# A kernel of eight fused layers on one core: the keys of the second full attention are computed inside the first cross attention, kept in DRAM and read back

## What is computed

```
x = x + L0_xattn(ln(x), ctx, mask)      # channels against channels, 16 heads of 8
x = x + L0_ffn(ln(x))                   # 8 experts, top 2
x = x + L1_xattn(ln(x), ctx)            # 16 heads of 16
x = x + L1_ffn(ln(x))                   # quantised, 256 -> 1024 -> 256
x = x + L2_xattn(ln(x), ctx)            # 16 heads of 128: q = ln(x) Wq, k = ctx Wk, v = ctx Wv
x = x + L2_ffn(ln(x))                   # LoRA experts
x = x + L3_xattn(ln(x), ctx, mask)      # memory readout
x = x + L3_ffn(ln(x))                   # grouped attention and 8 experts
```

## Time and profile before

| | us |
|---|---|
| median of three timed runs | 1279.91 |
| lowest and highest | 1278.62, 1280.27 |
| span of the profiled execution, first to last instruction | 1275.9 |
| what lies around the span, median less span | 4.0 |
| TensorE busy in the profile | 1085.1 |
| VectorE, ScalarE, GpSimd busy | 704.5, 503.4, 319.7 |

### The profile page before, as it was taken

The page is one execution under the profiler, slowest core; times in us unless marked ns, Lnnn a source line. Parts: engine busy times, 40 slices in busy tenths (PEclk is TensorE's granted clock), DMA queues, the critical chain, the costliest instruction groups (busy, mean ns, idle before and its releaser), DMA issues.

```text
span 1275.9 us, 20612 instructions
## 1 busy us (share of the span) xinstructions
PE 1085.1 (85%) x7154; PEld 830.8 (65%) x7170; DVE 704.5 (55%) x1700; ACT 503.4 (39%) x1785; POOL 319.7 (25%) x440
## 2 busy tenths in 40 slices
PE   1788886999996788799999999996788999984784
PEld 0355444899995566588888888884555666653463
DVE  5777756212223788854554455555656666665334
ACT  0165561233231466644333333342445555542121
POOL 5544211122322355510000000002222222210562
PEclk9699996899997799999999999998989999997797
DMA  6443207899882070000000000040000000000785
GB/s 185 133 129 110 84 32 237 301 327 334 315 322 79 10 256 1 2 28 20 1 1 1 1 1 1 34 133 1 1 1 9 5 6 5 5 4 24 238 250 177
DMA packets 59731, 121.31 MB, mean 95 GB/s; under 512 B 9049, under 2 KB 37481, under 8 KB 53713
## 3 DMA queue, kind: packets, MB, share of 16 engines
q1 hardware_dynamic: 52217, 106.62, 25.0%
q0 software_dynamic: 4416, 12.06, 2.8%
q10 hardware_dynamic: 2996, 1.32, 0.4%
HBM read 107.29 MB, written 12.49 MB: 94 GB/s over the span
## 4 chain that ended last, share of the span: by engine, by line
PE 60%; DVE 17%; issue 8%; ACT 7%; DMA 4%; POOL 2%; SPq 1%; another core or an unknown queue 1%; ACTq 0%; DVEq 0%; POOLq 0%
PE P L858 6%; PE P L868 6%; PE P L1789 4%; PE P L1782 4%; PE P L1834 4%; PE P L1798 4%; ACT big L2213 3%; DVE small L480 2%; PE P L1927 2%; PE P L1807 2%; PE P L1822 2%; PE P L1933 2%; PE P L1978 2%; ACT big L2181 2%; PE P L341 1%
## 5 line engine op out<-in xcount | busy, mean ns | idle before, releaser
L139 POOL TENSOR_TENSOR lrs<-lve,mhalf 128x1 f32<-128x1 f32 x64 | 36.6, 572 | 364.5 <-DVE lve L130 332.4
L480 DVE TENSOR_REDUCE small<-P 128x2 f32<-128x512 f32 x128 | 83.3, 681 | 38.9 <-PE P L305 38.2
L2124 ACT ACTIVATE big<-P,small 128x128 f32<-128x128 f32 x128 | 45.2, 366 | 145.0 <-DVE small L2304 145.0
L897 ACT ACTIVATE big<-P,big 128x128 f32<-128x128 f32 x184 | 52.5, 368 | 125.3 <-PE P L858 112.4
L556 ACT ACTIVATE big<-P 128x512 f32<-128x512 f32 x128 | 72.0, 598 | 58.6 <-PE P L323 53.6
L858 PE MATMUL P<-big 128*128 128x128 f32 x736 | 88.2, 279 | 0.1
L858 PEld LDWEIGHTS P<-big 128*128 128x128 f32 x736 | 86.1, 196 | 1.0 <-DMA big<-b_w 0.5
L868 PE MATMUL P<-big 128*128 128x256 f32 x368 | 83.1, 379 | 0.0
L305 PE MATMUL P<-big 90*128 90x256 bf16 x256 | 54.9, 303 | 32.9 <-DMA big<-scr_qk 17.5
L2295 DVE COPY big<-P 128x512 f32<-128x512 f32 x32 | 22.1, 692 | 107.2 <-PE P L1798 107.2
L999 DVE COPY big<-P 128x256 f32<-128x256 f32 x23 | 9.8, 425 | 125.3 <-PE P L868 125.3
(11 more groups left out here) (388 smaller groups left out, 2584.2 us busy)
## 6 DMA issues: line engine op xcount, KB each, us to landing
big<-b_w SPq DMA_DIRECT2D x23, 1028.0 KB
big<-b_w SPq DMA_DIRECT2D x23, 1024.0 KB
big<-scr_qk SPq DMA_DIRECT2D x96, 96.0 KB
big<-i_wgu SPq DMA_DIRECT2D x23, 352.0 KB
big<-moe_y SPq DMA_DIRECT2D x16, 256.0 KB, 4.2
big<-i_wd SPq DMA_DIRECT2D x23, 176.0 KB
scr_qk<-big SPq DMA_DIRECT2D x8, 384.0 KB
moe_x<-XN SPq DMA_DIRECT2D x16, 128.0 KB
```

Source lines behind the costliest of these rows:

```text
L480: dve.tensor_reduce(negM[:, h, :], P[:, h % 2, :].rearrange("p (c s) -> p c s", c=2), AX.X, ALU.max, negate=True).then_inc(a_max, 1)
```

## The change

The 32 parts of `k = ctx Wk` (128 head features by 512 tokens, four rows at once) are made by `key_part` in the first cross attention: parts 0 to 7 before its first step, parts 8 to 19 as halves of 256 columns in steps 0 to 23, parts 20 to 31 as halves in rows 2 to 7 at heads 5, 8, 11 and 14. ScalarE copies each part to SBUF (`key_take`) and stores it from its own queue (`key_store`, 256 KB in runs of 512 bytes). In the second full attention `keys4` and the copy to `e_k` are gone; each row's keys (1 MB) are read from DRAM into one of two buffers (`key_row`), and `e_q` has two buffers. Loads are rearranged for it: half of the context transposed and the first key weights come ahead of the remaining rows of `x` and `ctx`; `s0_behind` sends loads and mask rows behind the store of a row's queries and keys; the ACT queue carries rows 4 to 7 of `x` and one group of key weights. Loads of the grouped attention's weights wait for other counts, and semaphores are reused with an offset (a count of `e_ld` from 16 instead of 0, and the like), which are left out below.

```
@@ -210,6 +210,44 @@
+        k_wts = big1[:, 12288:16384].rearrange("p (g k n) -> p g k n", g=4, k=KD)
+        k_out = [XNT[:, s // 2, 512 * (s % 2):512 * (s % 2) + 512] for s in range(4)]
+        KEYS = nc.dram_tensor("keys_t", (B, 128, 4, 4, T), F32, kind="Internal").ap()
+        KP, K0, K1 = 32, 8, 20
+        def key_place(p):
+            g, rest = divmod(p, 8)
+            return g, rest // 4, rest % 4
+        def key_bank(p):
+            return 2 + p % 2 if p < K1 else 5
+        def key_weights(eng, g):
+            eng.dma_start(k_wts[:, g], e_wk.rearrange("(k p) n -> p k n", p=128)[:, :, 512 * g:512 * g + 512]
+                          ).then_inc(k_w[g], 16)
+        def key_take(act, p):
+            act.wait_ge(k_pe, p + 1)
+            if p >= 4:
+                act.wait_ge(k_st[p % 4], 16 * (p // 4))
+            act.activation(k_out[p % 4], P[:, key_bank(p), :], ACT.Copy).then_inc(k_ev, 1)
+        def key_store(act, p):
+            g, r, j = key_place(p)
+            act.wait_ge(k_ev, p + 1)
+            act.dma_start(KEYS[4 * r:4 * r + 4, :, g, j].rearrange("b p t -> p b t"),
+                          k_out[p % 4].rearrange("p (b t) -> p b t", b=4)).then_inc(k_st[p % 4], 16)
+        def late_pair(n, h):
+            if 2 <= n < B and h in (5, 8, 11, 14):
+                at = (5, 8, 11, 14).index(h)
+                return K1 + 2 * (n - 2) + at // 2, at % 2
+            return None
...
+            sp.dma_start(X[:, 2:4, :], x_cbt[:, 2:4, :]).then_inc(ld_x, 16)
+            ctx_t = ctxT.rearrange("(k p) n -> p k n", p=128)
+            sp.dma_start(CT[:, :, 0:512], ctx_t[:, :, 0:512]).then_inc(k_w[0], 16)
+            key_weights(sp, 0)
+            sp.dma_start(CT[:, :, 512:NT], ctx_t[:, :, 512:NT]).then_inc(k_ct, 16)
             sp.dma_start(idf[:, :], ident).then_inc(ld_id, 16)
-            sp.dma_start(X[:, 2:8, :], x_cbt[:, 2:8, :]).then_inc(ld_x, 16)
-            sp.dma_start(CX[:, 2:8, :], ctx_cbt[:, 2:8, :]).then_inc(ld_c, 16)
-            for dst, src in ((wvT, a_wvT), (bvb, rows(a_bv)), (tmT, maskT), (selm, a_sel),
-                             (TMf[:, 2 * D:], rows(mask_row[:, 2 * D:]))):
+            sp.dma_start(CX[:, 2:4, :], ctx_cbt[:, 2:4, :]).then_inc(ld_c, 16)
+            for dst, src in ((wvT, a_wvT), (bvb, rows(a_bv)), (tmT, maskT)):
...
+        def s0_behind(sp, n):
+            TMf = TM.rearrange("p b d -> p (b d)")
+            if n == 1:
+                sp.dma_start(TMf[:, 2 * D:], rows(mask.rearrange("b d -> (b d)").rearrange("(a n) -> a n", a=1)[:, 2 * D:])
+                             ).then_inc(a_ldm, 16)
+                sp.wait_ge(a_exd, 32)
+            if n in (1, 2):
+                for half in range(2):
+                    s0_extra(sp, n, half)
+            if n == 1:
+                key_weights(sp, 2)
+            if n == 2:
+                sp.dma_start(CX[:, 4:8, :], ctx.rearrange("b c t -> c b t")[:, 4:8, :]).then_inc(ld_c2, 16)
+                sp.dma_start(selm, a_sel).then_inc(a_ldm, 16)
+                key_weights(sp, 3)
...
+            def key_part(p, lo, hi):
+                g, r, j = key_place(p)
+                if lo == 0:
+                    if p % 8 == 0:
+                        pe.wait_ge(k_w[g], 32 if g == 0 else 16)
+                    if p == 4:
+                        pe.wait_ge(k_ct, 16)
+                    if p >= K1:
+                        pe.wait_ge(k_ev, p)
+                    elif p >= 2:
+                        pe.wait_ge(k_ev, p - 1)
+                for k in range(KD):
+                    t = pe.matmul(P[:, key_bank(p), lo:hi], k_wts[:, g, k, 128 * j:128 * j + 128],
+                                  CT[:, k, 512 * r + lo:512 * r + hi], start=(k == 0), stop=(k == KD - 1))
+                if hi == 512:
+                    t.then_inc(k_pe, 1)
             project(0)
             project(1)
+            for p in range(K0):
+                key_part(p, 0, 512)
             for step in range(STEPS):
                 n, h = divmod(step, H)
                 if n < B:
@@ -381,6 +469,13 @@
                 m, g = divmod(step - LEAD, H)
                 if 0 <= m < B:
                     turned(m, g)
+                if step < LEAD:
+                    key_part(K0 + step // 2, D * (step % 2), D * (step % 2) + D)
+                if late_pair(n, h) is not None:
+                    p, u = late_pair(n, h)
+                    if n + 2 < B and h == 5:
+                        pe.wait_ge(a_qb, n + 3)
+                    key_part(p, D * u, D * u + D)
...
+            key_take(act, 0)
+            key_store(act, 0)
+            act.dma_start(X[:, 4:8, :], x.rearrange("b c t -> c b t")[:, 4:8, :]).then_inc(ld_x2, 16)
+            key_take(act, 1)
+            key_store(act, 1)
+            key_weights(act, 1)
             act.wait_ge(a_exd, 32)
-            for n in range(3):
-                for half in range(2):
-                    s0_extra(act, n, half)
+            for p in range(2, K0):
+                if p in (2, 4):
+                    s0_extra(act, 0, p // 2 - 1)
+                key_take(act, p)
+                key_store(act, p)
...
+                if step < LEAD and step % 2:
+                    key_take(act, K0 + step // 2)
+                    key_store(act, K0 + step // 2)
                 if h == 3 and n + 2 < B:
                     queries_keys(n + 2)
                 if h == 4 and 0 < n <= B:
                     max_rows(n - 1)
                 if h == 7 and n < B:
                     values(n)
+                if 2 <= n < B and h in (9, 15):
+                    key_take(act, late_pair(n, h - 1)[0])
+                if 2 <= n < B and h == 11:
+                    key_store(act, late_pair(n, 8)[0])
+                if 3 <= n <= B and h == 1:
+                    key_store(act, late_pair(n - 1, 14)[0])
...
+        def key_row(sp, b):
+            if b >= 2:
+                sp.wait_ge(e_s, 4 * (b - 2) + 4)
+            sp.dma_start(e_kr[b % 2], KEYS[b]).then_inc(k_rd[b % 2], 16)
         def s4_sp(sp):
             sp.wait_ge(xn_ready, 3 * B)
-            for w, src in enumerate((e_wq, e_wk)):
-                for g in range(4):
-                    sp.dma_start(e_wqk[:, g, w], src.rearrange("(k p) n -> p k n", p=128)[:, :, 512 * g:512 * g + 512]
-                                 ).then_inc(e_ld, 16)
+            for signal in k_st:
+                sp.wait_ge(signal, 16 * KP // 4)
+            wq4 = e_wq.rearrange("(k p) n -> p k n", p=128)
+            sp.dma_start(e_wqs[:, 0], wq4[:, :, 0:512]).then_inc(e_ld, 16)
+            key_row(sp, 0)
+            for g in range(1, 4):
+                sp.dma_start(e_wqs[:, g], wq4[:, :, 512 * g:512 * g + 512]).then_inc(e_ld, 16)
             for g in range(4):
                 sp.dma_start(e_wvs[:, g], e_wv.rearrange("(k p) n -> p k n", p=128)[:, :, 512 * g:512 * g + 512]
                              ).then_inc(e_ld, 16)
             sp.dma_start(e_wos, e_wo.rearrange("(h p) d -> p h d", p=128)).then_inc(e_ld, 16)
+            key_row(sp, 1)
...
-            def keys4(m):
-                b, g = divmod(m, 4)
-                for j in range(4):
-                    for k in range(KD):
-                        t = pe.matmul(P[:, 1, j * T:j * T + T], e_wqk[:, g, 1, k, j * 128:j * 128 + 128],
-                                      CT[:, k, b * T:b * T + T], start=(k == 0), stop=(k == KD - 1))
...
             def scores4(m):
                 pe.wait_ge(e_qkT, m + 1)
+                b, g = divmod(m, 4)
+                if g == 0:
+                    pe.wait_ge(k_rd[b % 2], KRD0 + 16 * (b // 2) + 16)
                 if m >= 2:
                     pe.wait_ge(e_exp, m - 1)
                 for j in range(4):
-                    t = pe.matmul(P[:, 3 + m % 2, j * T:j * T + T], e_q[:, j, :], e_k[:, j, :], start=True, stop=True)
+                    t = pe.matmul(P[:, 3 + m % 2, j * T:j * T + T], e_q[m % 2][:, j, :], e_kr[b % 2][:, g, j, :],
+                                  start=True, stop=True)
                 t.then_inc(e_s, 1)
...
             def copy_qk4(m):
                 act.wait_ge(e_qk, m + 1)
-                if m > 0:
-                    act.wait_ge(e_s, m)
-                act.activation(e_q.rearrange("p j t -> p (j t)"), P[:, 0, :], ACT.Copy)
-                act.activation(e_k.rearrange("p j t -> p (j t)"), P[:, 1, :], ACT.Copy).then_inc(e_qkT, 1)
+                if m >= 2:
+                    act.wait_ge(e_s, m - 1)
+                act.activation(e_q[m % 2].rearrange("p j t -> p (j t)"), P[:, 0, :], ACT.Copy).then_inc(e_qkT, 1)
```

More of the change, by code:

```diff
@@ L285, in project @@
                     pe.wait_ge(ld_c, 16)
+                if n == 4:
+                    pe.wait_ge(ld_c2, 16)
+                if n >= 5:
+                    pe.wait_ge(k_ev, K1 + 2 * (n - 4))
                 pe.matmul(P[:, 5, 0:D], wqT, XN[:, n, :], start=True, stop=True)
@@ L746, in s1_sp0 @@
```

(33 more changed lines are left out.)

76 lines of the change are left out of this document (44 added, 32 removed).

## The result

The changed kernel takes 1271.72 us (median of four runs, 1269.50 to 1273.08) where the kernel before takes 1280.09 (1278.62 to 1281.80) on the same chip: a ratio of 0.9923, 95% interval 0.9901 to 0.9946. That is 8 us less. The forecast was 1236, with a range of 1224 to 1256. The sign was right; four fifths of the gain did not come.

A forecast was written before the change was run, and what follows sets the result against it. TensorE's work was taken to bound the full attention; in the first cross attention's later rows engines wait for each other. Full attention -54.8 and first attention +11.2 gave -43.6 from 1279.9: 1236 us, range 1224 to 1256.

The forecast's parts named there:

- Full attention, -54.8: Second full attention: removing `keys4` and the copy to `e_k` saves 54.8 us net, bounds 45 and 58.
- term of 3 us for side layers: Full attention: charge for shorter iterations uncovering waits, 8 rows at 0.2 us and the same again for what wasn't followed.
- ScalarE ... no bound: Before the first step: ScalarE's copies and stores (7 us) and mask-row DMAs (2.7) fit within TensorE's 10.3 us.
- So the parts end where the stack lands today: Before the first step: parts 0 to 7 take 17.2 us and end at 30.6, the stack landing at 30.9.
- head +2: Before the first step: the stack lands 2 us later behind added DMA traffic, bounds 0 and 6, or 10 at low clock.
- Steps 0 to 23, 30 us: First cross attention, steps 0 to 23: 30 us at full clock against 25.4, so +4.6; bounds 0 and +29.
- slower: the stores throttle the keys: Rival in head and steps: parts wait for store landings; 20 us per store costs 55 us more; chance of slower 0.02.
- Warm steps -2.2: First cross attention, steps 24 to 31: a TensorE at full clock gives back 2.2 of 6.9 us.
- Rows 2 to 7, +4.8: First cross attention: of four halves per row only head 8's is paid, 0.8 us a row; bounds 0 and 20.6.
- DMA +2: First cross attention, rows 2 to 7: late landings of stacks and maxima add 2 us, bounds 0 and 8.
- The rival at 1271 (half clock): Head and steps: clock stays at half, steps taking 54.9 us; +46 in the first attention, 1271 us, chance 0.04.

The follow-up runs named there:

- e7: Changed kernel with ScalarE's copy of the grouped layer's transposed rows ahead of the next exponentials and the probabilities' copy in the full attention: 1269.11 us, ratio 0.9898.
- e10: e8 plus e7's copy order, the last quarter of key weights issued later, and key halves of steps 16 to 19 behind the first maxima rows: 1236.77 us, ratio 0.9723.
- e3: Changed kernel with the 12 late key parts (rows 2 to 7) cut to one 64-column product each, copies and stores kept: 1268.44 us, ratio 0.9905.
- e4: Kernel before with only the full attention's part of the change, key rows read from `e_wk`, no keys computed or stored: 1231.09 us, ratio 0.9613.
- e8: e5 plus the wait for the small transfer moved to step 12 and stores 16 and 17 issued behind the first maxima rows: 1254.55 us, ratio 0.9792.
- e2: Changed kernel with each of the first 20 key stores sending one row of four (128 runs), the other rows' keys left out: 1258.44 us, ratio 0.9816.
- e5: Changed kernel with each key store writing 128 runs of 2 KB instead of 512 of 512 B, later reads in 512-byte runs: 1258.76 us, ratio 0.9824.

## Why the prediction was wrong

*Full attention, -54.8.* Right in kind: -47.1, TensorE-bound. The removed work was right. The term of 3 us for side layers was mis-sized: it was 10.7 (57.3 + 0.5 - 47.1). I looked at a normalised row, 0.2 us late, and "charge[d] the same again for what I haven't followed"; what I had not followed was ScalarE's copy behind the exponentials, 1.5 us once a row (e7: 6.4 us of it). The other 4.3 I did not trace.

*"ScalarE ... no bound", "So the parts end where the stack lands today", head +2.* This is the step that failed. I summed ScalarE's copies at 0.5 us and its issues at 0.68 each, and in that sum gave it no landing to wait for, though the diff shows the wait for `k_st` four parts later and the wait for `a_exd` behind eight parts. The stores were weighed by engine time (1.0 us each), which was right and beside the point: what counts for the engine that waits is the landing, 10.8 us in the median and up to 16.9, and the issue, up to 6 us. The measure I had for a landing was that of the stack's store in a quieter stretch (4.82). Parts 0 to 7 end at 38.9, not 30.6, and in the steps TensorE stands still from 46 to 60.85 for the copy of part 8.

*Steps 0 to 23, 30 us.* The term was mis-sized by its waits, not by its work: 1.09 us a step once they ran, at full clock (granted 1.00 in 66 to 82), as forecast, and 31.5 us of work; the other 21.8 of the 53.3 us are the waits above.

*The rival "slower: the stores throttle the keys".* It named the mechanism and got 0.02. It was set aside by asking when it would cost the whole gain (20 us a landing, all twenty parts), not what it costs at part of it. With landings of some 16 us in the head alone (16.9 and 16.0 for two stores, 15.9 for the small transfer) and issues of 6 it cost 35.9 us in head and steps, where 6.6 were forecast.

*Warm steps -2.2.* Hardly gained: from the first turned scores to the end of the first `weigh` it takes 6.6 us (92.27 to 98.88, granted clock 0.52), for 6.9 before (56.34 to 63.22). TensorE had stood still for 5.84 us before them in the changed kernel and for 0.53 in the one before, and a pair took 0.6 us from the start in both; in e10, after 1.59 us, it took 0.6 too, but only from 73.1 on. What brings the slower rate about was not varied by itself.

*Rows 2 to 7, +4.8.* Mis-sized: 7 us (e3). Three halves lie on the chain, not one.

*DMA +2.* No run shows this term. Without the halves the stretch takes 140.4 us (e3), and e4, without copies and stores either, 140.9. The small transfers of maxima land in 2.6 us (median, 99 to 219) where they took 2.2 before and 2.3 in e4 (70 to 172). So in the rows the trace shows 0.4 us more at most. In the steps it shows 8.23 for 3.24, and e8, with 6.7 us in the median whether two stores stood ahead of them or behind, says that the stores just ahead in the queue were not the cause.

*The sum.* Head and steps +35.9, rows +8.4, full attention -47.1, between +1.4, rest -3.2: -4.6 of span, against -43.6. The rest varies from 390.7 to 402.7 us among the traces, so the 3.2 in it say nothing. The rival at 1271 (half clock) gives the measured time by luck, for a wrong reason: the granted clock was 0.84 in the steps. (Its 54.9 us also leaves projections and `values` at full clock; doubled too, they make 57.5.)

*What stays open.* Whether the packets hold up ScalarE's own queue only, or each transfer: a second queue for the stores was not tried. Nor was the share of the loads that moved ahead (context, key weights, rows of `x`) taken out by itself: with quarter stores (e2) the first turned scores still come 18.1 us later than before, where 6.6 were forecast. In e10 they come 15.1 us later, of which 5.0 are the head's and 10.1 the steps'. TensorE works 32.4 of the steps' 35.6 us there, and its waits from the first part to the first turned scores are 10.1 us (4.2 for the stack, 3.3 for `key_take`, 1.6 for the maxima, 1.0 for VectorE), where the changed kernel has 29.6.

## What to carry to other kernels

For each transfer that a change adds, write down who waits for its landing and what stands behind that wait in an in-order stream; the engine time of the transfer did not show it here (1.0 us, worked out from the earlier trace rows, for a landing of 10.8 in the median). If the same engine issues stores, waits for them and makes the copies that feed TensorE, try few and long runs (here 128 of 2 KB for 512 of 512 B, the same bytes, gave 13 us) and give the short ones to the side that has time (here the later reads, which left the full attention at 286.9 us). When work leaves a stage bound by TensorE, look for every pair of TensorE instructions around it that are tied by another engine's copy: the work may have been its cover (here 1.5 us once a row), and putting the copy first in that engine's order gave 6.4 us back here (e7).

## What the runs showed of the hardware that I had not expected

Issuing a DMA is not a fixed 0.4 us: behind four stores of 512 packets one issue took 6.13 us, behind four of 128 packets 0.33. Stores of 256 KB landed in 10.8, 8.7 and 7.5 us in the median with 512, 256 and 128 packets, though the engines' busy share in 20 to 40 us was 0.86, 0.85 and 0.85. With 20 stores up to 100 us, ScalarE's queue had 12172 packets and took 25.0% of 16 engines; in e5, with 21 stores, it had 4780 packets and took 21.3%. So in engine time the longer runs saved little, and the 13 us that they gave are not engine time.
